# A two-layer cross-attention kernel: two output tiles of the last block but one moved behind the last block's logits, and three smaller moves

## The reference

```python
# layer 0 (16 heads of 64), x: (2, 2048, 512), ctx: (2, 128, 512)
qh, kh, vh = x @ Wq + bq, ctx @ Wk + bk, ctx @ Wv + bv        # by heads
attn = einsum('bqhd,bkhd->hbqk', qh, kh) * mask
attn = exp(attn - max(attn)) * mask                             # one maximum over everything
attn = attn / (sum(attn, axis=-1) + 1e-15)
y = layernorm(attn @ vh @ Wo + bo + x) * gamma + beta
# layer 1 (16 heads of 32)
q, k, v = y @ Wq.T, ctx @ Wk.T, ctx @ Wv.T                      # by heads
ctx1 = softmax(q k / sqrt(32)) v
out = layernorm(y + ctx1 @ Wo.T + bo) * ln_gamma + ln_beta
```

## Time and profile before

| | us |
|---|---|
| median of 3 runs | 914.35 |
| lowest and highest | 912.94, 914.93 |
| the profiled execution | 909.97 |
| its span, first to last instruction | 908.2 |

### The profile page before, as it was taken

How to read it: one execution, slowest core, us unless ns; L and a number is a source line. 1 busy time by engine, 2 the same in 40 slices (tenths; PEclk the granted TensorE clock), 3 DMA queues, 4 the chain that set the end, 5 groups by cost and what they waited for, 6 DMA issues and landing times.

```text
span 908.2 us, 11986 instructions
## 1 busy us (share of the span) xinstructions
PE 861.4 (95%) x4511; PEld 577.5 (64%) x4511; DVE 553.0 (61%) x1050; ACT 416.2 (46%) x560; POOL 456.1 (50%) x284
## 2 busy tenths in 40 slices
PE   7989999999999989989989999999999999999865
PEld 6567475665747464467577587576775875767624
DVE  1347565656657575877575656655756566556646
ACT  2325363645545354633543644535536345353440
POOL 0520404124040424327689588687795886863714
PEclk9999999999999999998999999999999999999968
DMA  9613335161514225973531432424314334210011
GB/s 349 247 62 136 124 121 200 47 245 51 197 70 177 108 94 214 290 265 95 131 101 47 140 93 93 140 70 137 119 47 139 93 93 139 70 70 1 1 47 47
DMA packets 47641, 111.55 MB, mean 123 GB/s; under 512 B 4704, under 2 KB 8544, under 8 KB 47584
## 3 DMA queue, kind: packets, MB, share of 16 engines
q1 hardware_dynamic: 47584, 110.78, 36.4%
HBM read 76.69 MB, written 34.08 MB: 122 GB/s over the span
## 4 chain that ended last, share of the span: by engine, by line
PE 81%; DVE 11%; POOL 3%; issue 2%; DMA 2%; ACT 1%; SPq 0%; POOLq 0%; DVEq 0%
PE bank L416 18%; PE bank L417 17%; PE bank L418 16%; PE bank L464 6%; PE bank L476 6%; PE bank L457 5%; PE bank L586 3%; PE bank L626 3%; DVE den L1123 2%; PE bank L410 2%; PE bank L404 2%; POOL a_lo L1318 2%; DVE r_hi L1127 1%; DMA r_first<-r_dram 1%; DVE scores L1014 1%
## 5 line engine op out<-in xcount | busy, mean ns | idle before, releaser
L416 PE MATMUL bank<-wo_lo,a_hi 128*128 128x512 f32 x384 | 156.0, 406 | 7.9 <-POOL a_lo L1435 3.9
L1280 POOL TENSOR_TENSOR x_lo<-x_raw,x_hi 128x2048 fp32r<-128x2048 f32 x8 | 39.0, 4878 | 235.1 <-ACT x_hi L774 235.1
L417 PE MATMUL bank<-wo_hi,a_lo 128*128 128x512 f32 x384 | 151.0, 393 | 0.0
L418 PE MATMUL bank<-wo_hi,a_hi 128*128 128x512 f32 x384 | 150.8, 393 | 0.0
L990 DVE CUSTOM_DVE_ANT_0 scores<-bank,mask_f 128x512 f32<-128x512 f32 x128 | 80.8, 688 | 58.1 <-PE bank L457 58.1
L862 ACT ACTIVATE scores<-scores,sh 128x512 f32<-128x512 f32 x128 | 80.3, 711 | 59.0 <-DVE sh L1116 59.0
L1313 POOL TENSOR_TENSOR a_lo<-a_raw,a_hi 128x1024 fp32r<-128x1024 f32 x32 | 80.0, 2503 | 52.8 <-ACT a_hi L843 52.8
L416 PE MATMUL bank<-x_lo,wq_hi 128*128 128x512 f32 x256 | 102.2, 399 | 3.9 <-DVE q_lo L981 3.0
L417 PE MATMUL bank<-x_hi,wq_lo 128*128 128x512 f32 x256 | 99.9, 390 | 0.0
L418 PE MATMUL bank<-x_hi,wq_hi 128*128 128x512 f32 x256 | 99.7, 390 | 0.0
L784 ACT ACTIVATE q_hi<-bank,bq_sb 128x512 fp32r<-128x512 f32 x64 | 44.1, 690 | 114.7 <-PE bank L418 112.0
(11 more groups left out here) (134 smaller groups left out, 1563.5 us busy)
## 6 DMA issues: line engine op xcount, KB each, us to landing
u_dram<-u_out SPq DMA_DIRECT2D x8, 2048.0 KB, 7.4
a_raw<-u_dram SPq DMA_DIRECT2D x32, 512.0 KB, 3.6
r_bc<-r_dram SPq DMA_DIRECT2D x56, 256.0 KB, 5.0
x_raw<-x_t SPq DMA_DIRECT2D x8, 1024.0 KB, 5.6
xn<-x_n SPq DMA_DIRECT2D x8, 1024.0 KB, 5.5
xb_dram<-xn SPq DMA_DIRECT2D x8, 1024.0 KB, 5.2
z<-xb_dram SPq DMA_DIRECT2D x32, 256.0 KB, 2.8
out<-z SPq DMA_DIRECT2D x7, 1024.0 KB, 6.7
```

The source lines that it names most:

```text
L416: nc.tensor.matmul(dst, lh, rl, start=first, stop=False)
L417: nc.tensor.matmul(dst, ll, rh, start=False, stop=False)
L418: return nc.tensor.matmul(dst, lh, rh, start=False, stop=last)
```

## The change

1. **The last iteration of PE.** Of block 6's four output1 tiles, the first stays, the second goes behind transposes 2 and 3 of block 7, and the third and fourth go behind the loop: behind logits1(7, 2) and behind logits1(7, 3) with its max_spread1. logits1(7, 3) goes ahead of max_spread1(7, 1).
2. **What follows from it.** Block 6's halves of the attention result get buffers of their own (a1_early_hi, a1_early_lo), the last block's z1 too (z1_last). Of block 6, rows1 and statistics of tiles 2 and 3, all moments, scales1, normal1, and POOL's out_scale and out_bias move behind block 7's last shift1; so does POOL's resid_scale and resid_bias for block 7's second half. Block 6's output is stored in halves between the tiles of block 7.
3. **The last block's low parts.** In each half POOL makes the low parts of columns 0 and 1, DVE those of columns 2 and 3. All four tiles are centered and scaled on DVE, and a tile is scaled one tile later than it is centered.
4. **ScalarE rounds layer 1's factors**: r1_hi is an activation on ACT between save_u1 and a0_high(i+1, 1), for blocks 0 to 6.
5. **Block 0.** rows0(0, 0) goes ahead of divisors0(2..5); divisors0(6, 7) goes behind the copies of v1. The four pieces of wq1_lo go behind moments0(0, 1) and moments0(0, 2), and PE waits for all four at queries1(0, 0). wo1_hi on ACT goes behind yt_high(0, 3). The first quarter of the query bias goes ahead of transposes 2 and 3. SP's store_r of blocks 2 to 7 goes behind the loads of block 1's first two tiles.

```diff
+               lambda k: (put(k, "a1_early_hi", [P, C1, QB], f32r), skip(k, 8),
+                         put(k, "a1_early_lo", [P, C1, QB], f32r)),
...
+               lambda k: (put(k, "resid z1", [P, QT, D]), put(k, "r_bc", [P, 2, TW])),
+               lambda k: (skip(k, 16), put(k, "z1_last", [P, QT, D])))
...
-               lambda k: (put(k, "wq1_hi wq1_lo", [P, KC, E1], f32r), put(k, "wo1_hi wo1_lo", [P, C1, D], f32r)))
+               lambda k: (put(k, "wq1_hi", [P, KC, E1], f32r), put(k, "wo1_hi", [P, C1, D], f32r),
+                         put(k, "wq1_lo", [P, KC, E1], f32r), put(k, "wo1_lo", [P, C1, D], f32r)))
...
+        def a1_split(i):
+            return (a1_early_hi, a1_early_lo) if i == NB - 2 else (a1_hi, a1_lo)
+        def z1_of(i):
+            return z1_last if i == NB - 1 else z1
...
@@ -366,18 +388,16 @@
             sp.wait_ge(rec_ready, 2)
             store_r(1)
             sp.wait_ge(r_stored, 16 * 2)
-            for i in range(2, NB - 1):
-                sp.wait_ge(rec_ready, i + 1)
-                store_r(i)
-            for i in range(NB + 1):
+            for i in range(NB):
                 more = i + 1 < NB
                 if more:
                     for n in (0, 1):
                         load_u(i + 1, n)
                         load_r(i + 1, n)
                 if i == 0:
-                    sp.wait_ge(rec_ready, NB)
-                    store_r(NB - 1)
+                    for b in range(2, NB):
+                        sp.wait_ge(rec_ready, b + 1)
+                        store_r(b)
...
-            for n in (1, 0, 2, 3):
-                sp.wait_ge(*((out_ready, 2 * (NB - 1) + 1) if n == 0 else (last_ready, n)))
-                sp.dma_start(out[NB - 1].rearrange("(t p) n -> p t n", p=P)[:, n, :],
-                             z1[:, n, :]).then_inc(out_stored, 16)
-            sp.wait_ge(out_stored, 16 * (NB - 1 + QT))
+            store_last(0)
+            store_half(NB - 2, 0)
+            store_last(1)
+            store_half(NB - 2, 1)
+            store_last(2)
+            store_last(3)
+            sp.wait_ge(out_stored, 16 * (NB - 2 + 2 + QT))
...
                 if i == 0:
                     pe.wait_ge(u_saved, (C0 + 1) * NB)
                     value_product(L_BANKS[1], wv1_sb, 1, 0).then_inc(kv1_psum_ready, 1)
+                    pe.wait_ge(w1_loaded, 32)
+                    query_bias(0)
                 if before:
                     output1(i - 1, 0)
+                if before and i < NB - 1:
                     output1(i - 1, 1)
                 transposes(i, 2)
                 transposes(i, 3)
                 if i == 0:
...
-                if before:
+                    for c in range(1, C1):
+                        query_bias(c)
+                    pe.wait_ge(wq1_ready, KC)
+                if i == NB - 1:
+                    output1(i - 1, 1)
+                elif before:
                     output1(i - 1, 2)
                 queries1(i, 0)
-                if before:
+                if before and i < NB - 1:
                     output1(i - 1, 3)
...
 
             i = NB - 1
+            output1(i - 1, 2)
             max_row1(i, 1)
+            logits1(i, 3)
             max_spread1(i, 1)
-            logits1(i, 3)
+            output1(i - 1, 3)
             sums1(i, 0)
...
+            def r1_high(i):
+                act.wait_ge(rec1_ready, i + 1)
+                act.wait_ge(u1_psum_ready, C1 * (i + 1))
+                nc.scalar.activation(r1_hi[:], den1[:], ACT.Copy).then_inc(r1_hi_ready, 1)
...
-                    act.wait_ge(xb_stored, 16 * NB)
-                    nc.scalar.activation(wo1_hi[:].rearrange("p c n -> p (c n)"), s_stage[:, 2048:4096],
-                                         ACT.Copy).then_inc(w1_hi_ready, 1)
                 normal0(i, 0)
                 normal0(i, 1)
...
                     for c in range(C1):
                         save_u1(i - 1, c)
+                    r1_high(i - 1)
                     if more:
...
                     a0_high(i + 1, 3)
                 if i == 0:
+                    act.wait_ge(kv1_psum_ready, C1 + B)
+                    nc.scalar.activation(wo1_hi[:].rearrange("p c n -> p (c n)"), s_stage[:, 2048:4096],
+                                         ACT.Copy).then_inc(w1_hi_ready, 1)
                     a0_high(1, 1)
...
             for c in range(C1):
                 save_u1(i, c)
+            for n in range(QT):
+                normal1(i - 1, n)
...
             factors0(slice(64, P), 0, 1, 2)
-            divisors0(2, 3, 4, 5)
-            factors0(slice(0, P), slice(1, 3), 4, 6)
-            divisors0(6)
-            factors0(slice(0, 64), 3, 1, 7)
+            def wq1_low(k):
+                if k == 0:
+                    dve.wait_ge(xb_stored, 16 * NB)
+                dve.wait_ge(w1_hi_ready, k + 1)
+                nc.vector.scalar_tensor_tensor(out=wq1_lo[:, k, :], in0=s_stage[:, k * E1:(k + 1) * E1],
+                                               scalar=g0_col[:, k:k + 1], in1=f(wq1_hi[:, k, :]),
+                                               op0=ALU.mult, op1=ALU.subtract).then_inc(wq1_ready, 1)
...
                 dve.wait_ge(rec1_ready, i + 1)
-                dve.wait_ge(u1_psum_ready, C1 * (i + 1))
-                nc.vector.tensor_copy(r1_hi[:], den1[:]).then_inc(r1_hi_ready, 1)
                 dve.wait_ge(r1_hi_ready, i + 1)
...
                     head_max(i - 1, 1)
                     shift1(i - 1, 1)
+                else:
+                    divisors0(2, 3, 4, 5)
+                    factors0(slice(0, P), slice(1, 3), 4, 6)
                 rows0(i, 1)
                 statistics0(i, 1)
                 moments0(i, 1)
                 if i == 0:
-                    divisors0(NB - 1)
-                    factors0(slice(64, P), NB // 2 - 1, 1, NB)
+                    wq1_low(0)
+                    wq1_low(1)
...
                 moments0(i, 2)
+                if i == 0:
+                    wq1_low(2)
+                    wq1_low(3)
...
                         nc.vector.tensor_copy(v1[:, b, :], L_BANKS[b][:]).then_inc(kv1_done, 1)
-                    for k in range(KC):
-                        last = nc.vector.scalar_tensor_tensor(out=wq1_lo[:, k, :], in0=s_stage[:, k * E1:(k + 1) * E1],
-                                                              scalar=g0_col[:, k:k + 1], in1=f(wq1_hi[:, k, :]),
-                                                              op0=ALU.mult, op1=ALU.subtract)
-                    last.then_inc(wq1_ready, 1)
+                    divisors0(6, 7)
+                    factors0(slice(0, P), 3, 2, NB)
...
-                if before:
+                if before and i < NB - 1:
                     rows1(i - 1, 3)
                     statistics1(i - 1, 3)
                     for n in range(QT):
                         moments1(i - 1, n)
-                else:
+                elif i == 0:
...
             shift1(i, 2)
+            for n in (2, 3):
+                rows1(i - 1, n)
+                statistics1(i - 1, n)
+            for n in range(QT):
+                moments1(i - 1, n)
             dve.wait_ge(sums1_psum_ready, NB)
             nc.vector.tensor_scalar(den1[:], SUM1_BANK[:], 1e-36, None, ALU.max).then_inc(den1_ready, 1)
             dve.wait_ge(den1_ready, NB)
-            dve.wait_ge(u1_psum_ready, C1 * NB)
             for half in range(2):
                 cols = slice(half * QB // 2, (half + 1) * QB // 2)
                 nc.vector.reciprocal(den1[:, cols], den1[:, cols]).then_inc(rec1_ready, 1)
                 dve.wait_ge(rec1_ready, NB + half)
+                dve.wait_ge(u1_psum_ready, C1 * NB)
                 nc.vector.tensor_copy(r1_hi[:, cols], den1[:, cols]).then_inc(r1_hi_ready, 1)
...
+                for c in range(2, C1):
+                    dve.wait_ge(a1_hi_ready, C1 * (i + half) + c + 1)
+                    nc.vector.tensor_tensor(a1_lo[:, c, cols], a1_raw[:, c, cols], f(a1_hi[:, c, cols]),
+                                            ALU.subtract).then_inc(a1_ready, 1)
+            def center_last(n):
+                dve.wait_ge(mv1_ready, QT * i + n + 1)
+                nc.vector.scalar_tensor_tensor(out=z1_last[:, n, :], in0=z1_last[:, n, :], scalar=mv1[:, n, 0:1],
+                                               in1=g1_b[:], op0=ALU.subtract, op1=ALU.mult).then_inc(last_centered, 1)
+            def scale_last(n):
+                dve.wait_ge(last_centered, n + 1)
+                dve.wait_ge(rstd1_ready, i + n + 1)
+                nc.vector.scalar_tensor_tensor(out=z1_last[:, n, :], in0=z1_last[:, n, :], scalar=rs1[:, n:n + 1],
+                                               in1=be1_b[:], op0=ALU.mult, op1=ALU.add).then_inc(last_ready, 1)
...
+                    scale_last(n - 1)
+            scale_last(QT - 1)
...
-                if before:
+                if before and more:
                     scales1(i - 1)
-                resid_scale(i, 1)
```

(22 more changed lines are left out.)

94 lines of the change are left out of this document (46 added, 48 removed).

## The result

The change takes 904.37 us, median of 4 runs (899.05 to 906.55), beside 914.24 for the kernel before on the same chip (912.94 to 914.93). The ratio is 0.989, 95% interval 0.985 to 0.993: 9.9 us faster. The forecast was 903.5, within 900 to 909.5. Further series beside other runs of before gave 912.32 (26 runs), 913.56 (11) and 912.14 (23) for before and 904.62 (6) for the change; beside the 912.32 the change is 7.7 us faster.

What follows compares the result with a forecast made beforehand. PE's own work bounds the kernel, so only its idle time can be won. Block 0 3.7 + ScalarE's rounding 1.0 + the end 6.2 = 10.9 us off: 903.5 us median, range 900 to 909.5.

Steps and rivals of the forecast that it cites:

- Block 0, 3.7 forecast: Block 0: PE's waits for z0 and yt_lo go, 3.85 us, but POOL's chain limits the lead kept to 3.7 us.
- Rival 1: Block 0's lead is lost because POOL or tile 2's load is late; block 0 keeps 0.5: 906.7 us; chance 0.17.
- ScalarE's rounding, 1.0 forecast: Iterations 2 to 6: rounding the factors on ACT saves 0.2 us each, 1.0 in all; nothing in iterations 1 and 7.
- (a): Block 7's logits: two moved output tiles fill the score waits and keep the clock up: 6.7 us off at the last sums.
- (b): Last block: POOL's wide residual steps hold DVE's cast and split of the factors: +2.7 us.
- (c): Last block: a half's four low parts shared by POOL and DVE: 1.0 us off, output1(7, 0) 5.0 earlier.
- (d): Last block's second half: the same 1.0 and part of a 0.76 wait, 6.3 us off at PE's last matmul.
- (e): Behind PE's last matmul: DVE's four tiles meet POOL's out_bias steps, 1.2 us taken, leaving 6.2 us off.
- Rival 2: At the end DVE's cast and split fall into gaps between POOL's steps and are not held: 900.8 us; chance 0.15.
- 3 (low parts over 2 us): Last block: DVE's second low part of each half waits behind a POOL wide step, twice 2.4: 908.3 us; chance 0.14.
- rival 4: Block 0's lead is lost and DVE's low parts at the end miss their turn: 911.5 us; chance 0.07.
- Rival 5: At the end POOL's six wide steps hold DVE steps and the scale pairs are exposed: slower, 918.4 us; chance 0.04.

Runs made afterwards that it cites:

- earlier r_bc: The changed kernel with SP's loads of r_bc for tiles 0 and 1 of block i+2 issued ahead of the loads of z: 899.14 us.
- the second course: Block 0 with a lower clock from 410 to 420 us and PE later, in the changed kernel with resid_last (901.46 us) or second-half low parts on POOL (901.80).
- the end alone: The kernel before with only the change's part for the end, without block 0's part or ScalarE's rounding: 907.95 us.
- the residual's own buffer: The changed kernel with a separate buffer, resid_last, for the second half of the last block's residual: 901.46 us.
- block 0's part and the rounding: The kernel before with the change's block 0 part and ScalarE's rounding of the factors, nothing at the end: 908.08 us.

## Why the prediction was right, and where not

**The total.** 904.37 beside 903.5. From output0(0, 0) the executions say 8.5 us less, the medians 9.9 and 7.7, of 10.9 forecast. So the forecast was too high by 1 to 3 us. That it looks as near as 0.9 us is in part luck: the kernel before stood at 914.24 in that series, at 912.1 to 913.6 in the others. By parts it was 1.9 too high for block 0, 0.5 too low for the rounding and 1.0 too high for the end.

**Block 0, 3.7 forecast, 1.8 measured.** PE's own part was right in kind and too small: both waits went, the query bias, which was to stay, took 1.0 less, and queries1(0, 0) came 5.7 earlier where 3.9 was forecast. The bound by POOL's chain was right in size too (3.8 at POOL's first multiplication, 4.0 at the split's end). The step that failed stands behind it: "I take 3.7" let PE keep all of POOL's gain, and nothing was set down for the clock behind the wait of a PE that comes too early. It got to the split 6.0 us earlier, waited 4.2, and the clock halved behind the wait; from the split to the second reciprocal it then took 56.5 us instead of 54.3 (before: 54.35): 4.0 less 2.2 is the 1.8. The run with earlier r_bc gets back the clock's 2.2 and 3.6 more at the split. A second thing was not seen: wo_lo stands behind queries1(0, 0) on DVE and moved up by 5.5 us, POOL's multiplication by 3.7, so their order turned, which held POOL by 2.1 us. The two profiles of the change and the two of the second course differ by 3.3 to 4.0 us at the second reciprocal; 2.1 to 2.6 of that is the clock, the rest the earlier split. Rival 1 had named the sign, a new wait over 3 us in iteration 1, but not its cause: neither the move of POOL nor SP's stores. SP's loads behind the stores were issued at 415.1, 30.3 us behind output0(0, 0), where I had put them (412, 30.9); in the change that cost nothing, but four of the other profiles show POOL waiting 0.4 to 1.3 us for r_bc of that tile.

**ScalarE's rounding, 1.0 forecast, 1.5 measured in iterations 2 to 6.** 0.3 each instead of 0.2. ACT took 0.63, inside the 0.43 to 1 that I gave it. The split is indeed held (1.72), and PE's wait for POOL's low parts took its place (2.1 us in five waits). In iteration 1 "nothing" was wrong: ACT's r_hi stands behind an a_hi that waits for POOL. Whether DVE's cast would have come sooner there, with PE as early, no run shows.

**The end, 6.2 forecast, 5.2 measured.** The second profiles of the two kernels say 5.5, the end alone 5.8 or 6.2, so a part of the missing 1.0 is scatter. By its terms, all behind the seventh reciprocal:

- (a) 6.7 at the last sums; measured 6.8 (den at 49.83 instead of 56.63).
- (b) +2.7 for cast and split; measured +2.2, at the split's end 4.8 less. It was there, as the residual's own buffer shows. This trace agrees with the rule of the Trainium skill (SBUF — State Buffer, Who interferes with whom) that was weighed: 2.52 us beside POOL's step, 0.48 without it. The rows of wo_lo show the same in both orders of start.
- (c) 1.0 at the first output1; measured 0.9 (59.0 against 59.8). With (a) and (b) that tile came 5.65 us earlier, where 5.0 was forecast.
- (d) 6.3 at PE's last matmul, 1.3 more than at the first output1; measured 5.8, 0.1 more (with the end alone 0.5 more). This term was mis-sized. The second half's low parts do come earlier behind their a_raw, but in front of output1(7, 2) PE now waits 0.56 for DVE's z_last, the add that stands behind DVE's own two low parts. With that half's four low parts on POOL PE ends as soon (73.9 for 74.0).
- (e) 6.2 at the end; measured 5.2. This was mis-sized too: DVE's tail behind PE's last matmul was to grow by 0.1 and grew by 0.5, in the other three profiles with this end too (8.1 to 8.2 us, of 7.6). From the second half's a_raw DVE has almost no gap (0.16 us, and 0.51 before the last scaling), so that what is taken from it counts: its two low parts of that half (1.30) and two centrings held by POOL's out_bias (1.65 and 1.62 for 0.75). Giving back the low parts shortened this chain by 0.9, and F by 0.8 to 1.4 against the four profiles with the change's end.

**Rivals.** Rival 2 (DVE not held) and 3 (low parts over 2 us) are excluded by 2.52 and by 1.29 and 1.30 for two low parts each, and rival 4 with them. Rival 5 is excluded: of six wide steps, three held a DVE step on which the end waited, together 4.0 us (2.2 in cast and split, 0.9 in each of two centrings); the second split's 2.0 beside out_scale was hidden behind PE. Rival 1's number holds in half, 1.8 of 3.7 kept, by another way than its own: iteration 1 did not start late.

## What to carry to other kernels

A lead is worth what the next engine can take: follow it to the first wait behind it, through the in-order queue of the engine that has been given the new step, and price that wait with the clock that falls behind it. When an engine's work moves by a few microseconds, ask which pairs of steps that lock each other change their order of start, since whichever begins second pays. Sharing work between two engines is only a gain where the one that takes it has a gap; look at what sets the end behind it.

## What the runs showed of the hardware that I had not expected

- In iteration 1 the waits of 4.2 to 5.7 us were followed by a fall of the clock to 0.50 in all four profiles that had them (a mean of 0.83 from 455 to 475 us); waits of 2.2 us and less were not (1.00 in nine profiles), except once (0.91, 1.9 us, with the end alone). The fall cost 2.1 to 2.6 us up to the second reciprocal in the four, 1.4 in the one.
- How long the clock stays down behind the same waits differs between executions. Before and the run with block 0's part and the rounding have the same code and the same waits at the end (for low parts, scores and the split: 3.9, 3.6 or 3.7, and 2.8 us). Stretches of 2 us, first of before, then of that run (PE busy, granted clock, DMA share, GB/s):

```profile
861.00:863.00 2.00, 1.01 (x7) 0.50 0.00 0
863.00:865.00 2.00, 2.00 (x16) 0.50 0.00 0
865.00:867.00 2.00, 1.30 (x8) 0.50 0.94 367
867.00:869.00 2.00, 1.85 (x9) 0.50 0.42 158
869.00:871.00 2.00, 2.00 (x14) 0.50 0.03 8
```

```profile
861.00:863.00 2.00, 2.00 (x18) 0.51 0.00 0
863.00:865.00 2.00, 1.72 (x8) 0.64 0.58 227
865.00:867.00 2.00, 1.29 (x10) 1.00 0.77 297
```

  The end (F) was 1.8 us shorter by it, as much as one of the change's terms. The other three profiles with that code at the end have 89.8 to 90.2 us, as before. Whether that is what scatters the runs of before (906.3 to 918.6 us in one series, against 898.8 to 900.3 with earlier r_bc) no run tells.
- In the change the reads of r_bc for block 2, 256 KB each, landed 8 us after their issue (the median of four). They were issued behind four loads of z and among two of u (512 KB each), which landed in 2.7 and 7.7 us.
